# Recurrent stage of a decoder: the turned items regrouped into one row set and two channel groups

## The chip, the cores and the metric

The kernel runs on one core of a Trainium2 chip. The metric is the device time of one execution in microseconds. The five engines (TensorE or PE, VectorE or DVE, ScalarE or ACT, GpSimd or POOL, SyncE or SP) run their own instruction lists strictly in order and meet through semaphores; SyncE issues the transfers.

## The reference, cut to what matters

A two-layer decoder over 8 sequences of 256 tokens and 128 channels. Layer 0: linear attention, cross attention, a quantised feed-forward. Layer 1: four selective-scan (Mamba) blocks, cross attention with 16 heads of 64, a mixture of experts. Only the scan blocks matter here:

```python
dt = softplus(dbl[..., :64] @ dtw + dtb)
Bm, Cm = dbl[..., 64:80], dbl[..., 80:96]
A = -exp(A_log)
dA = exp(dt[..., None] * A)
dBu = (dt * u)[..., None] * Bm[:, :, None, :]
h = dA_t * h + dBu_t
y = einsum('ben,bn->be', h, C_t)
```

There are 256 inner channels and 16 states per channel, so each token has 4096 recurrences per block.

## The kernel before, in words

All of the change lies in `mamba_stage` (L1563 on). The work is cut into 16 **rounds** f (4 blocks times 4 quarters of 512 tokens, that is two sequences). While round f scans, the same engines prepare round F = f + 1 (projections, silu, softplus) and normalise the input of G = f + 2.

The 256 x 16 recurrences of a round are 16 **items** k, t = k % 16 being the place in the round. An item is a tile of 128 partitions x 1024: each partition holds one channel of a group of four (E32 = 32 channels by NI = 4 states), and the 1024 columns are two rows of 512 tokens. `place(k)` (L1604) says which: before, item t has channel half h = t // 8, row set pair np = (t // 4) % 2 and channel group q = t % 4; its two rows are two row sets of B and C (of NO = 4) for one channel group. Rows of dt and dt*u for the half are spread over the partitions by DMA (`dtR`, `dtuR`), rows of B and C likewise (`Bt`, `Ct`).

For an item the engines do: ScalarE `decay` (L2000), two exponentials of 512 columns with a scale per partition, into a PSUM pair that alternates by k % 2, so decay k waits for item k-2 to be done with its pair. GpSimd `times_b` (L1776), dt*u times B into one of eight slots of `hs`, three items ahead. VectorE `scan` (L2189), 1024 columns. Then the product with C, `times_c`, on VectorE for 9 items of a round (`NORM_D`, L1581) and on GpSimd (L1788) for the other 7: t = 0, 5, 9 to 13. TensorE `sum_y(f, j)` (L1861) folds the four items of batch j into a PSUM bank `Y[h]`, 8 matmuls, once all four products are there; VectorE `gate` multiplies the result of a half with silu(z).

Four items, t = 12 to 15, are **turned**: no GpSimd times_b. ScalarE makes scaled copies of the transposed dt*u (`scale_rows`, L2038, one per 128 tokens, state and row set: 32 a round, spread over the steps by `SCALED`), TensorE transposes them into the PSUM pair (`turn_rows`, L1914, 8 transposes an item), ScalarE writes their decays into `hs`, without a wait for the pair. `turn_b`/`copy_b` and `turn_dtu`/`copy_dtu` (L1900, L2025, L1906, L2032) make the transposed B and dt*u of the next round.

The order is written out by hand. ScalarE (L2124 on) does at step t: decay t+1, then what is due: `silus(F)` at 2 (two table loads, four silus), `x_rows` at 3, the softplus at 5, 6, 7, `copy_b` at 9, `square(G)` at 10, `residual(f-1)` at 11, `inv_std(G)` at 12, `affine(G)` at 14, `copy_dtu` at 15; then its scaled copies; then, at `KV_AT` = 4, 7, 12, 14 (L1654), one `kv_copy` (L2019): four times a round a tile of the next stage's keys or values, made by TensorE in a spare bank (`kv_job`, L1878), is brought to SBUF. VectorE (L2209) does scan, product, and `gate(f-1,1)` at 1, `step_size(F)` at 8, `gate(f,0)` at 9, `scaled_x(G)` at 13. GpSimd (L1805) does times_b t+3, times_c t, and `dt_times_u(F)` (L1794) at 8. TensorE's list (L1930 on) is, for a round: tap projection 0, sum_y(f-1,3), skip 0, tap projection 1, gate projection 0 (waits for `gate(f-1,1)`), gate projection 1 (waits for the first silu), x projection, kv_job, sum_y(f,0), dt projection, kv_job, sum_y(f,1), skip 1, turn_b (waits for `step_size`), centre(G), out_projection(f-1) (waits for `copy_b`), kv_job, turn_rows 12, average(G) (waits for `residual(f-1)`, since both use bank PA), turn_rows 13, sum_y(f,2), turn_rows 14, kv_job, turn_rows 15, turn_dtu.

## Time and profile before

| what | us |
|---|---|
| median of 3 runs | 1713.18 (1711.62 to 1714.34) |
| profiled execution, its own time | 1711.71 |
| its span, first to last instruction | 1710.0 |
| first scan starts, last product ends (in the span) | 501.86, 1318.14 |
| DVE busy over the span | 1387.7 |
| ACT busy over the span | 1312.0 |
| POOL busy over the span | 1074.3 |
| PE busy over the span | 1342.9 |

Busy times are sums of instruction durations on one engine; the clock of TensorE is given as a share of 2.4 GHz. In a timeline, "x2" merges instructions of one line and form that follow each other; the bracket is the engine's idle time before the row and what ended it. Round 8 (910.61 to 961.34) stands for the others: scan 0 of each round starts 50.7 us after the one before.

### The profile page before, as it was taken

The numbers are of one execution on the slowest core, as the hardware profiler recorded it, in microseconds if no ns is written. First come the engines' busy times: TensorE is split into PE (matmuls) and PEld (weight loads), VectorE is DVE, ScalarE is ACT, GpSimd is POOL, SyncE is SP. The second block draws the span as 40 slices with busy tenths as digits, with TensorE's granted clock in tenths as the row PEclk, the third lists the DMA queues.
The fourth block names the chain that finished last, engine by engine and source line by source line (L and its number), as shares of the span: only waits on it lengthen the run. The fifth ranks groups of instructions, "written<-read, shape, count | busy, mean of one in ns | idle before, by whom it ended". The sixth has DMA issues, their size and how long they took to land. (4 is left out here: it accounts for less than half of the span.)

```text
span 1710.0 us, 25211 instructions
## 1 busy us (share of the span) xinstructions
PE 1342.9 (79%) x7544; PEld 697.8 (41%) x7547; DVE 1387.7 (81%) x2394; ACT 1312.0 (77%) x2978; POOL 1074.3 (63%) x714
## 2 busy tenths in 40 slices
PE   6777898996677777877777777767766999899989
PEld 4554555653322222332222333222322466566543
DVE  3655788896529999999999999999997688778834
ACT  4444787884658999999999999999975787777730
POOL 2001566661048999999999999999995344444500
PEclk9999899998978889999988988999977999999979
DMA  3000000001045534455434545443530511121000
GB/s 105 2 1 2 1 2 2 1 2 26 7 174 203 179 124 173 167 205 199 168 136 162 203 157 199 177 160 129 192 142 25 185 50 50 62 87 50 2 0 25
DMA packets 70229, 168.19 MB, mean 98 GB/s; under 512 B 20420, under 2 KB 40152, under 8 KB 56664
## 3 DMA queue, kind: packets, MB, share of 16 engines
q1 hardware_dynamic: 68680, 166.17, 26.9%
q8 instruction: 55, 0.90, 0.2%
q10 hardware_dynamic: 1168, 0.53, 0.1%
q14 instruction: 70, 0.57, 0.1%
q0 software_dynamic: 256, 0.01, 0.0%
HBM read 131.04 MB, written 35.65 MB: 97 GB/s over the span
## 5 line engine op out<-in xcount | busy, mean ns | idle before, releaser
L1784 POOL TENSOR_TENSOR ma_hs<-ma_dtuR,ma_Bt 128x1024 f32<-128x1024 f32 x192 | 449.4, 2375 | 12.7 <-DMA ma_dtuR<-ma_dtu_d 6.7
L914 POOL TENSOR_TENSOR x_pr<-x_pr,x_rec 128x512 f32<-128x512 f32 x256 | 267.4, 1045 | 248.1 <-DVE x_rec L1202 248.1
L1161 ACT ACTIVATE x_pr<-x_sm,x_mx 128x256 f32<-128x256 f32 x512 | 255.3, 500 | 68.8 <-DVE x_mx L1193 65.7
L1867 PE MATMUL ps<-ma_hs,ma_fold 128*32 128x512 f32 x1024 | 157.7, 744 | 179.2 <-DVE ma_hs L2203 172.2
L2015 ACT ACTIVATE ps<-ma_dtR,ma_A 128x512 f32<-128x512 f32 x384 | 248.6, 680 | 48.6 <-DVE ma_hs L2203 41.6
L1792 POOL TENSOR_TENSOR ma_hs<-ma_hs,ma_Ct 128x1024 f32<-128x1024 f32 x112 | 264.3, 2371 | 22.2 <-DVE ma_hs L2197 22.2
L2197 DVE TENSOR_TENSOR_SCAN ps<-ps,ma_hs 128x1024 f32<-128x1024 f32 x112 | 255.9, 2285 | 7.9 <-ACT ps L2015 7.9
L2045 ACT ACTIVATE ma_rowB<-ma_dtuT,ma_BT 128x128 f32<-128x128 f32 x512 | 232.6, 524 | 1.3
L2197 DVE TENSOR_TENSOR_SCAN ma_hs<-ps,ma_hs 128x1024 f32<-128x1024 f32 x80 | 180.7, 2275 | 5.1 <-ACT ps L2015 5.1
L2203 DVE TENSOR_TENSOR ma_hs<-ps,ma_Ct 128x1024 f32<-128x1024 f32 x144 | 176.2, 1224 | 5.0
L990 PE MATMUL ps<-ident,x_pr 128*128 128x128 f32 x1024 | 161.6, 283 | 5.7 <-DVE x_pT L1073 4.3
L1867 PEld LDWEIGHTS ps<-ma_hs,ma_fold 128*32 128x32 f32 x1024 | 31.5, 125 | 274.3 <-DVE ma_hs L2203 210.5
L990 PEld LDWEIGHTS ps<-ident,x_pr 128*128 128x128 f32 x1024 | 113.2, 141 | 73.2 <-issue 52.9
L1193 DVE CUSTOM_DVE_ANT_0 x_sm<-x_sm,x_neg 128x256 f32<-128x256 f32 x256 | 111.6, 471 | 24.4 <-DVE x_sm L1189 24.4
L1834 PE MATMUL ps<-ma_hn,ma_w_tap 128*128 128x512 f32 (+3 forms) x256 | 118.6, 608 | 3.2 <-ACT ma_hn L2062 3.2
L1193 DVE CUSTOM_DVE_ANT_0 x_sm<-ps,x_mr 128x256 f32<-128x256 f32 x256 | 97.5, 418 | 22.4 <-PE ps L978 16.8
L1189 DVE TENSOR_TENSOR x_sm<-ps,x_m 128x512 f32<-128x512 f32 x128 | 86.6, 677 | 25.9 <-PE ps L978 25.5
L1161 ACT ACTIVATION_READ_ACCUMULATOR x_pr<-x_sm,x_mx 128x1 f32 x512 | 96.4, 188 | 0.0
L1073 DVE COPY x_pT<-ps 128x512 f32<-128x512 f32 x128 | 86.5, 676 | 5.0 <-PE ps L990 4.6
L1075 ACT ACTIVATE x_pT<-ps 128x512 f32<-128x512 f32 x128 | 74.7, 584 | 15.8 <-PE ps L990 14.3
L2015 ACT ACTIVATE ma_hs<-ma_dtR,ma_A 128x512 f32<-128x512 f32 x128 | 83.4, 716 | 0.0
L713 DVE TENSOR_TENSOR la_sc<-ps,la_tri 128x512 f32<-128x512 f32 x64 | 43.3, 680 | 48.2 <-PE ps L496 48.2
(325 smaller groups left out, 2598.8 us busy)
## 6 DMA issues: line engine op xcount, KB each, us to landing
ma_dtuR<-ma_dtu_d SPq DMA_DIRECT2D x32, 1024.0 KB, 6.7
ma_dtR<-ma_dt_d SPq DMA_DIRECT2D x32, 1024.0 KB, 6.6
ma_Bt<-ma_bc_d SPq DMA_DIRECT2D x16, 1024.0 KB, 4.9
ma_Ct<-ma_bc_d SPq DMA_DIRECT2D x16, 1024.0 KB, 7.4
ma_dtu_d<-ma_dtu SPq DMA_DIRECT2D x32, 256.0 KB, 2.0
ma_dt_d<-ma_dt SPq DMA_DIRECT2D x32, 256.0 KB, 2.3
keys_d<-ma_kv SPq DMA_DIRECT2D x32, 256.0 KB, 2.6
values_d<-ma_kv SPq DMA_DIRECT2D x32, 256.0 KB, 2.5
```

The costliest lines, as they stand in the source:

```text
L914: pool.tensor_tensor(pr[:, r, :, :], pr[:, r, :, :], rec[:, r, :].unsqueeze(2).broadcast_to([P, 2, L]), ALU.mult).then_inc(pr_done, 1)
L990: mm = pe.transpose(c.ps[:, 2 + n % 2, kt * L + t * P:kt * L + (t + 1) * P], pr[:, n % RP, t, kt * P:(kt + 1) * P], c.ident[:, :])
L1161: a = act.activation(pr[:, n % RP, t, :], sm[:, n % 2, t, :], ACT.Exp, bias=mx[:, n % 2, t:t + 1], scale=-1.0, accum_out=den[:, n % RP, t: ...
L1193: a = dve.tensor_tensor_reduce(sm[:, n % 2, t, :], bank[:, t, :] if small else sm[:, n % 2, t, :], mr[:, p, :] if small else neg[:, t, :], ...
L1784: pool.tensor_tensor(hs[:, k % SLOTS, :, :], dtuR[:, h, q, :].unsqueeze(1).broadcast_to([P, 2, CH]), rows(Bt, k), ALU.mult).then_inc(dbu_d ...
L1792: pool.tensor_tensor(hs[:, k % SLOTS, :, :], hs[:, k % SLOTS, :, :], rows(Ct, k), ALU.mult).then_inc(c_pool, 1)
L1834: mm = pe.matmul(out, w_tap[:, b, TAPS - 1 - e, h * P:(h + 1) * P], src, start=(e == 0), stop=(e == TAPS - 1), skip_group_check=True)
L1867: mm = pe.matmul(c.ps[q * E32:(q + 1) * E32, Y[h], :], fold[:, :], hs[:, (k0 + q) % SLOTS, a, :], start=False, stop=(j % 2 == 1 and a == 1 ...
L2015: e = act.activation(hs[:, k % SLOTS, a, :] if by_tensor(k) else c.ps[:, 2 * (k % 2) + a, :], dtR[:, h, q, :], ACT.Exp, scale=A[:, (f // Q ...
L2045: act.activation(rowB[:, t, a, :, :, ni], dtuT[:, t, :].rearrange("p (e q) -> p q e", q=GQ), ACT.Copy, scale=BT[:, f % 2, t, a, ni:ni + 1] ...
L2197: dve.tensor_tensor_scan(out, decays, inputs, 0.0, ALU.mult, ALU.add).then_inc(scan_done, 1)
L2203: dve.tensor_tensor(hs[:, k % SLOTS, :, :], c.ps[:, 2 * (k % 2):2 * (k % 2) + 2, :], rows(Ct, k), ALU.mult).then_inc(c_vector, 1)
```

## The change

- **Items.** An item is now one row set no and two channel groups (2qp, 2qp+1) of a half: `dtuR` gives two rows, B and C one row used twice. `ORDER` lists them: six items of half 0 (no 0 to 2), four of half 1 (no 0, 1), two of half 0 (no 3), four of half 1 (no 2, 3).
- **Turned items** are t = 10, 11 (half 0, no = 3) and 14, 15 (half 1, no = 3). All four use one row set, so 16 scaled copies of 256 columns (both halves) replace 32 of 128; `SCALED` spreads them over t = 0 to 8 and 15. `turn_dtu` transposes both halves into PA and PB (8 transposes), `copy_dtu` copies 1024 columns, at t = 14. `Bt` keeps three row sets.
- **Who makes the product with C**: GpSimd now for t = 0, 6, 8, 9, 12, 13, 14.
- **kv tiles**: copied at t = 0, 1, 4, 6; two jobs use Y[0] before skip 0, two Y[1] before skip 1. The two stores that stood behind Bt and Ct on SP's queue stand ahead of the wait for x_rows.
- **gate(f,0)** moves from t = 9 to t = 14, after sum_y(f,2), since half 0 now ends with item 11.
- TensorE's list follows; tap projection 0 now waits for `copy_dtu`.

```diff
@@ -1578,9 +1579,13 @@
     BIG = 1.0e24
-    NORM_D = set(range(16)) - {0, 5, 9, 10, 11, 12, 13}
-    TURNED = {12, 13, 14, 15}
-    SCALED = (3, 4, 0, 1, 2, 3, 3, 3, 3, 4, 3, 0, 0, 0, 0, 3)
+    NORM_D = set(range(16)) - {0, 6, 8, 9, 12, 13, 14}
+    TURNED = {10, 11, 14, 15}
+    SCALED = (2, 2, 0, 3, 2, 1, 0, 1, 2, 0, 0, 0, 0, 0, 0, 3)
+    FIRST, LAST_B, LAST = (0, 6), (5, 13), (11, 15)
+    ORDER = tuple((0, no, qp) for no in range(3) for qp in range(2)) + ((1, 0, 0), (1, 0, 1), (1, 1, 0), (1, 1, 1),
+                                                                        (0, 3, 0), (0, 3, 1), (1, 2, 0), (1, 2, 1),
+                                                                        (1, 3, 0), (1, 3, 1))
     xm = c.xn
@@ -1602,8 +1607,7 @@
-        s = k % ITEMS
-        return k // ITEMS, s // 8, (s // 4) % 2, s % 4
+        return (k // ITEMS,) + ORDER[k % ITEMS]
@@ -1620,10 +1624,10 @@
-        dtuT = s.sb("dtuT", [P, 4, P])
-        BT = s.sb("BT", [P, 2, 4, 2, NI])
+        dtuT = s.sb("dtuT", [P, 2, 4, P])
+        BT = s.sb("BT", [P, 2, 4, NI])
...
-        Bt = s.sb("Bt", [P, 2, NO, CH])
+        Bt = s.sb("Bt", [P, 2, NO - 1, CH])
@@ -1651,7 +1655,8 @@
         KV_K = 32
-        KV_AT = (4, 7, 12, 14)
+        KV_AT = (0, 1, 4, 6)
+        KV_BANK = (Y[0], Y[0], Y[1], Y[1])

@@ -1684,8 +1689,8 @@
-            f, _, np_, _ = place(k)
-            return tile[:, f % 2, 2 * np_:2 * np_ + 2, :]
+            f, _, no, _ = place(k)
+            return tile[:, f % 2, no, :].unsqueeze(1).broadcast_to([P, 2, CH])
@@ -1715,18 +1720,19 @@
+                    if f >= 0:
+                        kv_store(sp, 4 * f)
+                        kv_store(sp, 4 * f + 1)
...
+                        used = (NO - 1 + k) * CH
...
-                                     .broadcast_to([E32, NI, NO * CH])).then_inc(done, 16)
-                    if f >= 0:
-                        kv_store(sp, 4 * f)
-                        kv_store(sp, 4 * f + 1)
+                                     [:, :, 0:used].broadcast_to([E32, NI, used])).then_inc(done, 16)
@@ -1738,19 +1744,19 @@
-                        sp.wait_ge(dbu_done, n_times_b(f * ITEMS + 8))
+                        sp.wait_ge(dbu_done, n_times_b(f * ITEMS + LAST_B[0] + 1))
...
-                        sp.wait_ge(da_done, f * ITEMS + 8)
+                        sp.wait_ge(da_done, f * ITEMS + LAST[0] + 1)
...
-                        sp.wait_ge(dbu_done, n_times_b(f * ITEMS + 16))
+                        sp.wait_ge(dbu_done, n_times_b(f * ITEMS + LAST_B[1] + 1))
...
-                        sp.wait_ge(da_done, f * ITEMS + 16)
+                        sp.wait_ge(da_done, f * ITEMS + LAST[1] + 1)
@@ -1774,15 +1780,15 @@
-                    f, h, np_, q = place(k)
+                    f, h, _, qp = place(k)
...
-                    if k % 8 == 0:
+                    if k % ITEMS == FIRST[h]:
...
-                                       dtuR[:, h, q, :].unsqueeze(1).broadcast_to([P, 2, CH]),
+                                       dtuR[:, h, 2 * qp:2 * qp + 2, :],
@@ -1859,13 +1865,14 @@
-                    h = j // 2
...
-                    for a in range(2):
-                        for q in range(GQ):
-                            mm = pe.matmul(c.ps[q * E32:(q + 1) * E32, Y[h], :], fold[:, :], hs[:, (k0 + q) % SLOTS, a, :],
-                                           start=False, stop=(j % 2 == 1 and a == 1), skip_group_check=True)
+                    for k in range(k0, k0 + 4):
+                        _, h, _, qp = place(k)
+                        for a in range(2):
+                            q = 2 * qp + a
+                            mm = pe.matmul(c.ps[q * E32:(q + 1) * E32, Y[h], :], fold[:, :], hs[:, k % SLOTS, a, :],
+                                           start=False, stop=(k % ITEMS in (LAST[h] - 1, LAST[h])), skip_group_check=True)
@@ -1905,15 +1912,19 @@
                     if F + 1 < NF:
+                        pe.wait_ge(lnv_done, F + 2)
                         pe.wait_ge(scaled, F + 2)
+                    else:
+                        pe.wait_ge(resid, F - 1)
                     pe.wait_ge(dtu_done, 2 * F + 2)
-                    for a in range(4):
-                        mm = pe.transpose(c.ps[:, PB, a * P:(a + 1) * P], dtu[:, 1, a * P:(a + 1) * P], c.ident[:, :])
+                    for h, bank in ((0, PA), (1, PB)):
+                        for a in range(4):
+                            mm = pe.transpose(c.ps[:, bank, a * P:(a + 1) * P], dtu[:, h, a * P:(a + 1) * P], c.ident[:, :])
                     mm.then_inc(dtuT_ps, 1)
...
                 def turn_rows(k):
-                    f, h, np_, q = place(k)
-                    pe.wait_ge(rows_done, 32 * (f + 1))
+                    f, h, _, qp = place(k)
+                    pe.wait_ge(rows_done, 16 * (f + 1))
                     if on_vector(k - 2):
@@ -1921,7 +1932,7 @@
                             mm = pe.transpose(c.ps[:, 2 * (k % 2) + a, t * P:(t + 1) * P],
-                                              rowB[:, t, a, q, :, :].rearrange("p e n -> p (e n)"), c.ident[:, :])
+                                              rowB[:, t, h, 2 * qp + a, :, :].rearrange("p e n -> p (e n)"), c.ident[:, :])
                     mm.then_inc(turned, 1)
@@ -1930,40 +1941,45 @@
                 for f in range(-1, NF + 1):
                     F, G = f + 1, f + 2
                     if F < NF:
+                        if f >= 0:
+                            pe.wait_ge(dtuT_done, f + 1)
                         tap_projection(F, 0, PA)
                     if f >= 1:
                         sum_y(f - 1, 3)
                     if 0 <= f < NF:
-                        pe.wait_ge(dd_done, 2 * (f // QUARTERS) + 2)
                         if f >= 1:
                             pe.wait_ge(gated, 2 * f - 1)
-                            pe.wait_ge(kv_done, 4 * f)
-                        skip(f, 0)
+                        kv_job(4 * f, Y[0])
                     if F < NF:
-                        if f >= 0:
-                            pe.wait_ge(dtuT_done, f + 1)
                         tap_projection(F, 1, PB)
                         if f >= 1:
                             pe.wait_ge(gated, 2 * f)
                         gate_projection(F, 0, Y[1])
+                    if 0 <= f < NF:
+                        pe.wait_ge(kv_done, 4 * f + 1)
+                        kv_job(4 * f + 1, Y[0])
+                    if F < NF:
                         pe.wait_ge(u_done, 2 * F + 1)
                         gate_projection(F, 1, PA)
                         x_projection(F)
                     if 0 <= f < NF:
+                        pe.wait_ge(dd_done, 2 * (f // QUARTERS) + 2)
+                        pe.wait_ge(kv_done, 4 * f + 2)
+                        skip(f, 0)
                         if F < NF:
                             pe.wait_ge(z_done, 2 * F + 1)
                         else:
                             pe.wait_ge(gated, 2 * f)
-                        kv_job(4 * f, Y[1])
+                        kv_job(4 * f + 2, Y[1])
                         sum_y(f, 0)
                     if F < NF:
                         dt_projection(F)
                     if 0 <= f < NF:
-                        pe.wait_ge(kv_done, 4 * f + 1)
-                        kv_job(4 * f + 1, Y[1])
+                        pe.wait_ge(kv_done, 4 * f + 3)
+                        kv_job(4 * f + 3, Y[1])
+                        pe.wait_ge(kv_done, 4 * f + 4)
+                        skip(f, 1)
                         sum_y(f, 1)
-                        pe.wait_ge(kv_done, 4 * f + 2)
-                        skip(f, 1)
                     if F < NF:
                         pe.wait_ge(dt_done, 2 * F + 2)
                         turn_b(F)
@@ -1976,30 +1992,25 @@
                             pe.wait_ge(resid, f - 1)
                         out_projection(f - 1)
                     if 0 <= f < NF:
-                        pe.wait_ge(gated, 2 * f + 1)
-                        kv_job(4 * f + 2, Y[0])
-                    if 0 <= f < NF:
-                        turn_rows(f * ITEMS + 12)
+                        turn_rows(f * ITEMS + 10)
                     if G < NF:
                         if f >= 1:
                             pe.wait_ge(resid, f)
                         average(G)
                     if 0 <= f < NF:
-                        turn_rows(f * ITEMS + 13)
+                        turn_rows(f * ITEMS + 11)
                         sum_y(f, 2)
                         turn_rows(f * ITEMS + 14)
-                        pe.wait_ge(kv_done, 4 * f + 3)
-                        kv_job(4 * f + 3, Y[0])
+                    if F < NF:
+                        turn_dtu(F)
                     if 0 <= f < NF:
                         turn_rows(f * ITEMS + 15)
-                    if F < NF:
-                        turn_dtu(F)

             @block.scalar
             def _(act):
                 def decay(k):
-                    f, h, np_, q = place(k)
-                    if k % 8 == 0:
+                    f, h, no, qp = place(k)
+                    if k % ITEMS == FIRST[h]:
                         act.wait_ge(dt_in[h], 16 * (f + 1))
                     if k % (ITEMS * QUARTERS) == 0:
                         act.wait_ge(a_done, f // QUARTERS + 1)
@@ -2011,7 +2022,7 @@
-                        no = 2 * np_ + a
+                        q = 2 * qp + a
@@ -2025,15 +2036,16 @@
-                        act.wait_ge(rows_done, 32 * (F - 1))
-                    act.activation(BT[:, F % 2, :, :, :], c.ps[:, PA, 0:4 * 2 * NS].rearrange("p (t x n o) -> p t x o n", t=4, x=2, o=NO)
-                                   [:, :, 0, 2:4, :], ACT.Copy).then_inc(bT_done, 1)
+                        act.wait_ge(rows_done, 16 * (F - 1))
+                    act.activation(BT[:, F % 2, :, :], c.ps[:, PA, 0:4 * 2 * NS].rearrange("p (t x n o) -> p t x o n", t=4, x=2, o=NO)
+                                   [:, :, 0, NO - 1, :], ACT.Copy).then_inc(bT_done, 1)
...
-                        act.wait_ge(rows_done, 32 * F)
-                    act.activation(dtuT[:, :, :].rearrange("p t e -> p (t e)"), c.ps[:, PB, :], ACT.Copy).then_inc(dtuT_done, 1)
+                        act.wait_ge(rows_done, 16 * F)
+                    act.activation(dtuT[:, :, :, :].rearrange("p h t e -> p h (t e)"), c.ps[:, PA:PB + 1, :], ACT.Copy
+                                   ).then_inc(dtuT_done, 1)
@@ -2041,9 +2053,9 @@
-                    t, a, ni = i // 8, i // 4 % 2, i % 4
-                    act.activation(rowB[:, t, a, :, :, ni], dtuT[:, t, :].rearrange("p (e q) -> p q e", q=GQ), ACT.Copy,
-                                   scale=BT[:, f % 2, t, a, ni:ni + 1]).then_inc(rows_done, 1)
+                    t, ni = divmod(i, 4)
+                    act.activation(rowB[:, t, :, :, :, ni], dtuT[:, :, t, :].rearrange("p h (e q) -> p h q e", q=GQ), ACT.Copy,
+                                   scale=BT[:, f % 2, t, ni:ni + 1]).then_inc(rows_done, 1)
@@ -2150,7 +2162,7 @@
                             copy_b(F)
-                        if F < NF and t == 15:
+                        if F < NF and t == 14:
                             copy_dtu(F)
@@ -2161,7 +2173,7 @@
                         if t in KV_AT:
-                            kv_copy(4 * f + KV_AT.index(t), Y[1] if t < 9 else Y[0])
+                            kv_copy(4 * f + KV_AT.index(t), KV_BANK[KV_AT.index(t)])
                         if t == 14 and f % QUARTERS == 1 and f // QUARTERS + 1 < NBLK:
@@ -2182,7 +2194,7 @@
                 def gate(f, h):
-                    dve.wait_ge(y_done, 4 * f + 2 * h + 2)
+                    dve.wait_ge(y_done, 4 * f + h + 3)
                     zz = z[:, f % 3, h, :]
@@ -2220,10 +2232,10 @@
                             step_size(F)
-                        if t == 9:
-                            gate(f, 0)
                         if t == 13 and G < NF:
                             scaled_x(G)
+                        if t == 14:
+                            gate(f, 0)

```

## Rows read from the trace of the kernel before

**Rows 1.** The page, part 1: busy us of each engine, share of the span, instructions.

```profile
PE 1342.9 (79%) x7544; PEld 697.8 (41%) x7547; DVE 1387.7 (81%) x2394; ACT 1312.0 (77%) x2978; POOL 1074.3 (63%) x714
```

**Rows 2.** Windows: length, busy time and count by engine, clock, DMA share, GB/s.

```profile
911.80:962.50 50.70, 37.62 (x161) 14.98 (x154) 49.48 (x31) 47.57 (x87) 46.91 (x24) 0.90 0.49 180
```

**Rows 3.** Timeline of VectorE, round 8: start, duration, line, out<-in, [idle before <-releaser].

```profile
910.61 2.28 DVE L2197 TENSOR_TENSOR_SCAN ma_hs<-ps,ma_hs 128x1024 f32<-128x1024 f32 x1
912.81 2.27 DVE L2197 TENSOR_TENSOR_SCAN ps<-ps,ma_hs 128x1024 f32<-128x1024 f32 x1
...
916.26 0.68 DVE L2187 TENSOR_TENSOR ma_z<-ps,ma_z 128x512 f32<-128x512 f32 x1
...
924.20 2.30 DVE L2197 TENSOR_TENSOR_SCAN ps<-ps,ma_hs 128x1024 f32<-128x1024 f32 x1 [0.34 <-ACT ps L2015]
...
941.44 2.28 DVE L2197 TENSOR_TENSOR_SCAN ma_hs<-ps,ma_hs 128x1024 f32<-128x1024 f32 x1
...
954.40 2.29 DVE L2197 TENSOR_TENSOR_SCAN ps<-ma_hs,ps 128x1024 f32<-128x1024 f32 x1 [0.36 <-PE ps L1923]
...
957.87 2.29 DVE L2197 TENSOR_TENSOR_SCAN ps<-ma_hs,ps 128x1024 f32<-128x1024 f32 x1
...
961.34 2.28 DVE L2197 TENSOR_TENSOR_SCAN ma_hs<-ps,ma_hs 128x1024 f32<-128x1024 f32 x1
```

**Rows 4.** Timeline of ScalarE, round 8.

```profile
909.25 1.35 ACT L2045 ACTIVATE ma_rowB<-ma_dtuT,ma_BT 128x128 f32<-128x128 f32 x3
...
916.37 1.30 ACT L2015 ACTIVATE ps<-ma_dtR,ma_A 128x512 f32<-128x512 f32 x2
...
922.80 1.30 ACT L2015 ACTIVATE ps<-ma_dtR,ma_A 128x512 f32<-128x512 f32 x2
...
927.01 0.59 ACT L2023 ACTIVATE ma_kv<-ps 128x512 f32<-128x512 f32 x1
```

**Rows 5.** Timeline of TensorE, round 8; a product counts twice or more.

```profile
910.75 1.92 PE L1867 MATMUL ps<-ma_hs,ma_fold 128*32 128x512 f32 x16 [1.52 <-DVE ma_hs L2203]
...
913.57 3.58 PE L1834 MATMUL ps<-ma_hn,ma_w_tap 128*128 128x512 f32 x8
916.99 1.13 PE L1840 MATMUL ps<-ma_hn,ma_w_gate 128*128 128x512 f32 x2
...
936.92 3.64 PE L1867 MATMUL ps<-ma_hs,ma_fold 128*32 128x512 f32 x16 [8.14 <-DVE ma_hs L2203]
...
942.10 0.43 PE L1902 MATMUL ps<-ident,ma_xp 32*128 32x32 f32 x4
...
945.99 1.02 PE L1888 MATMUL ps<-ma_w_kv,cT 128*128 128x512 f32 x2
947.43 1.09 PE L1923 MATMUL ps<-ident,ma_rowB 128*128 128x128 f32 x8 [0.42 <-ACT ma_rowB L2045]
949.14 1.12 PE L1898 MATMUL ps<-ma_sq,average 128*128 128x512 f32 x2 [0.61 <-ACT xn L2083]
```

**Rows 6.** ScalarE by form: count, busy us, mean ns of one, idle before.

```profile
L2045 ACT ACTIVATE ma_rowB<-ma_dtuT,ma_BT 128x128 f32<-128x128 f32 x512 | 232.6, 524 | 1.3
...
L590 ACT ACTIVATE la_qm<-la_qk,la_member 128x256 f32<-128x256 f32 x64 | 28.4, 499 | 0.0
...
L1406 ACT ACTIVATE ffn_y<-ps,ffn_ht 128x128 f32<-128x128 f32 x16 | 5.1, 382 | 1.2 <-PE ps L1350 1.2
```

**Rows 7.** Timeline of GpSimd, round 8.

```profile
946.58 7.05 POOL L1792 TENSOR_TENSOR ma_hs<-ma_hs,ma_Ct 128x1024 f32<-128x1024 f32 x3 [0.41 <-DVE ma_hs L2197]
...
958.23 4.70 POOL L1784 TENSOR_TENSOR ma_hs<-ma_dtuR,ma_Bt 128x1024 f32<-128x1024 f32 x2
```

**Rows 8.** Timelines of TensorE (rounds 0 and 15) and VectorE (round 14).

```profile
512.36 2.08 PE L1840 MATMUL ps<-ma_hn,ma_w_gate 128*128 128x512 f32 x2 [4.02 <-ACT ma_u L2069]
...
1267.46 3.64 PE L1867 MATMUL ps<-ma_hs,ma_fold 128*32 128x512 f32 x16 [4.94 <-DVE ma_hs L2203]
...
1260.39 2.29 DVE L2197 TENSOR_TENSOR_SCAN ps<-ma_hs,ps 128x1024 f32<-128x1024 f32 x1 [2.94 <-PE ps L1923]
```

## The prediction

> **What bounds the kernel now.** I read the page first: VectorE is the busiest engine [rows 1]. Then the windows: in one round of the recurrent stage (0.8 ms of the span, sixteen rounds) VectorE is busy 49.48 of 50.70 us, ScalarE 47.57, GpSimd 46.91, TensorE 37.62 [rows 2]. So VectorE's list of sixteen scans sets the pace, and what can be won is its idle time alone, some 1.2 us a round. The timeline of VectorE shows where that sits [rows 3]: 0.34 us ahead of scan 4, released by ScalarE, and 0.55 us ahead of the turned scans, 0.36 of it ahead of scan 14, released by TensorE. An item whose product VectorE makes takes it 3.46 us (957.87 to 961.34), one whose product GpSimd makes 2.20 (910.61 to 912.81), a gate 0.6. Every microsecond by which another engine makes VectorE wait is lost for good. Round 8 is the pattern; T is the start of scan 0 (910.61), S the end of `step_size` (941.44, T + 30.8), X the start of scan 11.
>
> ScalarE's timeline says why scan 4 waits [rows 4]: decay 3 starts at T + 5.8, then come two table loads and four silus, decay 4 starts 6.43 us after decay 3 (922.80 - 916.37), and scan 4 follows its start by 1.40. TensorE takes its list strictly in order: it sits 8.14 us idle before `sum_y(1)`, whose first matmuls then last 3.64 us where 1.92 is usual [rows 5]. The granted clock averages 0.90 of 2.4 GHz over the round [rows 2]: a fifth of it ran at the lower level of 1.2 GHz, and that is where it lies.
>
> **Part 1: the scaled copies.** 32 copies of 128 columns a round become 16 of 256. One takes 524 ns, three take 1.35 us together [rows 4, 6]. A copy of 256 contiguous columns with a scale of the same kind takes 499 ns, one of 128 takes 382 [rows 6]; so the 256 strided ones lie between 0.45 us apiece and twice the old one, 0.9. I take 0.55, nearest to the old row plus the difference of the other two. ScalarE's busy time falls by 14.5 (232.6 / 16) - 8.8 = 5.7 us a round (bounds 0 and 7.3). ScalarE does not bound the round, so this is worth at most the 0.34 us ahead of scan 4, and only if nothing else makes decay 4 late. The Trainium skill (SBUF — State Buffer, section Door 1, the note on cachelines) says that consecutive accesses that each cross to a new 16-byte line pay a penalty. The copies step by 16 bytes on both sides; the excess of 524 over 382 ns agrees, and if that penalty is paid per element a copy would cost about 0.7 us by that rule, an estimate; only three copies lie on the path below, so the sum would move by under 0.5 us a round.
>
> **Part 2: kv copies at t = 0 and 1.** They were behind decays 5, 8, 13 and 15, where ScalarE had slack; now the first two stand before decay 2 and decay 3 in ScalarE's list.
> (a) kv_job 4f stands behind `sum_y(f-1,3)`, and that waits for item 14's product on GpSimd. Its list after scan 12 is now product 12, times_b 16, product 13, times_b 17, product 14: five instructions of 2.33 us [rows 7], 11.7 us from the end of scan 12 at X + 5.65, thus X + 17.3. Scan 0 of the next round would start at X + 14.7 (items 11 and 15 at 3.46, 12 to 14 at 2.20, a gate and a `scaled_x` at 0.6). So `sum_y` starts at T + 2.7 (before: T + 0.1), takes 1.9, the job 1.0, the copy 0.5 [rows 4, 5]: decay 2 starts at T + 6.2, scan 2 at T + 7.6 where it was 6.25.
> (b) kv_job 4f+1 stands behind the second tap projection (3.4) and behind a gate projection (1.0), which waits for `gate(f-1,1)` (done at T + 6.3). From T + 5.6: tap to 9.1, gate projection to 10.0, job to 11.1, copy to 11.6. Decay 3 starts there (before 5.8), scan 3 at T + 13.0, decay 4 at 11.6 + 6.43 = 18.0, scan 4 at T + 19.4 instead of 13.6.
> (c) TensorE is then idle from 11.1 until the first silu ends at 14.9, 3.8 us. In the first round it was idle 4.02 us there, and its gate projection took 2.08 instead of 1.13 us [rows 5, 8]. That adds 0.93: scan 4 at T + 20.35. Three copies and `x_rows` between decays 4 and 5 add 0.2. Together **7.0 us** later at S than now (5.8 with the clock at its upper level).
>
> **Part 3: the turned items are 10, 11, 14, 15 (were 12 to 15).** Their transposes stand where the old ones stood in TensorE's list.
> (a) `turn_rows(10)` is behind turn_b, centre and out_projection(f-1). turn_b waits for `step_size`, and with `sum_y(1)` at its 3.64 us it starts at S + 0.3. From turn_b to the end of out_projection is 945.99 - 942.10 = 3.9 us, the transposes 1.09 [rows 5]: scan 10 can start at S + 5.3. VectorE has only scan 9 to do after S and is free at S + 2.2. Before, four scans and a gate stood there. **3.1 us** lost.
> (b) `turn_rows(11)` is behind average(G), and that waits for residual(f-1) [rows 5], which on ScalarE stands behind decay 12. Decay 12 is now an ordinary one, so it waits for item 10's product: S + 5.3 + 3.46 = 8.8. Then decay 12 (1.2), residual (0.6, as the kv copy of rows 4), average (1.0) and transposes (1.0): scan 11 at S + 12.8, VectorE free at 8.8: 4.0 us. TensorE was idle 5.4 us before average; each idle of 4.9 us and more in this stage was followed by matmuls at the lower level [rows 5, 8]. With that, average and transposes take 2.0 us more: **5.9 us**.
> (c) After X, `turn_rows(14)` and `turn_rows(15)` are ready at X + 6.7 to 8.8 and X + 10.6 to 12 against VectorE's X + 8.45 and 11.25: 0.4 us. The 0.57 us that the turned scans waited before is gone.
>
> **Part 4: with one answer.** Scans (16), VectorE products (9), times_b (12) and GpSimd products (7) keep number and shape, the scan at 2.28, GpSimd's at 2.35 us [rows 3, 7]; a repeated row in place of two rows costs nothing, since times_b repeats one operand already and takes as long as the product that doesn't. `turn_dtu` has 8 transposes for 4 and `copy_dtu` 1024 columns for 512, each 0.5 us, before T and under scans 14 and 15. Bt's load is a quarter smaller; DMA engines are busy about half [rows 2]. On SP's queue dtR 0 now waits for decay 11, at S + 2.3, under the wait for dtu anyway; dtuR 1 waits for times_b 13 at S + 11, and is needed a round later; the kv stores that moved ahead of `xp_done` are done by then. If these were late, decay 16 or times_b 16 would wait; there are over 5 us of room.
>
> **Sum.** A full round (f = 1 to 13): 7.0 + 3.1 + 5.9 + 0.4 - 0.6 = 15.8, times 13 = 205. Round 0: 4.5 (no sum to wait for, but tap 0 now waits for copy_dtu). Round 14: 7.0 + 3.1 + 1.2 less the 2.94 us stall of before [rows 8] = 8.4. Round 15: 2.5 (no taps, no silus). Opening: 1. That is +221 us on the profiled execution's 1711.7: 1933. The median of the runs is 1.5 us above it, so 1934. About 0.2% (3 us) is what a measurement of this kernel tells from nothing.
>
> **Rivals.**
> - *The clock holds* at 2.4 GHz through the idle times of 3.8 and 5.4 us: 5.8 + 3.1 + 4.0 - 0.6 = 12.3 a round, 160 + 12: 1885. Against it: rows 8.
> - *The clock also falls in the 3.2 us before `sum_y(3)`*: sum and job 1.7 + 1.0 us longer, ahead of decay 3: 2.7 to 3.5 a round, 14 rounds: 1972 to 1982. For it: the shortest idle time followed by the lower level in this stage is 4.02, against it 1.5 us did no harm; nothing lies between.
> - *Only one of the two groups of waits holds* (part 2 hidden, or part 3): 13 x 8.8 + 5 gives 1833, 13 x 6.4 + 15 gives 1812. It needs an error of mine in one engine's order.
> - *Faster*: the halved copies take ScalarE out of the way, decay 4 comes early, and both stalls of rows 3 vanish: 16 x 1.0 + 2.9 + 1 = 20, 1694. This decides if the first two kv copies are ready when ScalarE comes to them, that is if kv_job 4f+1 ends by T + 5.2, one copy ahead of decay 3's start. Against it: it cannot start before the gate at T + 6.3. The Trainium skill (Perfetto Trace Analysis, Optimizing Scalar/DVE Operations) holds that fewer, larger operations raise throughput if the engine is saturated; at 47.57 of 50.70 us ScalarE is close to it, which is what speaks for this case.
> - *It changes nothing*: the copies gain what the waits cost: 1713.
>
> **How the numbers follow.** Forecast 0.50; clock holds 0.15; clock falls earlier too 0.22; one group only 0.07; faster 0.04; nothing 0.02. The forecast is the likeliest. Leaving out the last three (0.13) and little above 1985, the range is 1850 to 1985; its lower end lets 35 us of waits be smaller than in the clock-holds case. Faster 0.04, same 0.02, slower 0.94.
>
> **What would show it.** The page: VectorE busy time as before (1388 us), the span some 220 longer. VectorE's timeline in a middle round: period 66 us; idle ahead of scan 2 and 3 (1.4, 1.9), scan 4 (3 to 4) from ScalarE; ahead of scan 10 (3.1) and scan 11 (5.9) from TensorE's transposes. ScalarE: idle ahead of the kv copies, released by TensorE. The copies at L2045: 256 of them, near 0.6 us. TensorE's clock at 0.5 at average. Wrong if scan 11 follows scan 10's product at once, if the period is under 60 us, or if VectorE's own instructions got longer.

## The result, and the profile after

The changed kernel takes 1939.95 us (median of 4 runs, 1938.44 to 1940.37) against 1713.76 for the kernel before (4 runs): ratio 1.1321, 95% interval 1.1306 to 1.1336. The forecast was 1934, so the change is slower by what was said, within 6 us. The profiled execution took 1938.44, against 1711.71: +226.7 where the sum gave +221.

The page of the changed kernel, busy times (its row of [rows 1]):

```profile
PE 1446.3 (75%) x7608; PEld 743.0 (38%) x7611; DVE 1395.7 (72%) x2394; ACT 1274.3 (66%) x2722; POOL 1073.9 (55%) x714
```

ScalarE has 37.7 us less to do (1312.0 - 1274.3): 51.4 less in scaled copies, less what the doubled `copy_dtu` takes and what the records lose in overlap. GpSimd has the same. TensorE has 64 transposes more, four a round in `turn_dtu`, and is busy 103 us longer, most of it because more of its matmuls ran at the lower clock: the granted clock over the span is 0.871, against 0.922 before. VectorE's busy time is 8.0 us longer. 3.0 of that is in the durations of its instructions, which add up to 1532.6 us against 1529.6; the other 5 come from the records, in which an instruction that follows its predecessor at once overlaps it by some 0.08 us (in round 8 scan 1 starts at 1033.45, 0.09 us before scan 0 ends) and one that waited does not. Nearly all of the 227 us is idle time of VectorE.

The groups of VectorE by line, shapes apart, for the kernel before (count, busy us, mean ns, idle time just before them and what ended it):

```profile
L2197 DVE TENSOR_TENSOR_SCAN ps<-ps,ma_hs 128x1024 f32<-128x1024 f32 x112 | 255.9, 2285 | 7.9 <-ACT ps L2015 7.9
...
L2197 DVE TENSOR_TENSOR_SCAN ps<-ma_hs,ps 128x1024 f32<-128x1024 f32 x32 | 73.3, 2290 | 10.9 <-PE ps L1923 8.9 <-ACT ma_hs L2015 1.7
L2197 DVE TENSOR_TENSOR_SCAN ma_hs<-ma_hs,ps 128x1024 f32<-128x1024 f32 x32 | 72.7, 2277 | 4.5 <-PE ps L1923 1.9 <-ACT ma_hs L2015 1.7
```

The same groups of the changed kernel:

```profile
L2209 DVE TENSOR_TENSOR_SCAN ps<-ps,ma_hs 128x1024 f32<-128x1024 f32 x96 | 220.2, 2294 | 116.3 <-ACT ps L2026 110.7 <-POOL ma_hs L1790 3.8
...
L2209 DVE TENSOR_TENSOR_SCAN ps<-ma_hs,ps 128x1024 f32<-128x1024 f32 x48 | 110.0, 2291 | 118.2 <-PE ps L1934 118.2
...
L2209 DVE TENSOR_TENSOR_SCAN ma_hs<-ma_hs,ps 128x1024 f32<-128x1024 f32 x16 | 36.5, 2284 | 4.4 <-PE ps L1934 4.1
```

"ps<-ps,ma_hs" are ordinary items whose product VectorE makes: idle time ahead of them rises from 7.9 to 116.3 us, released by ScalarE's decays. "ps<-ma_hs,ps" and "ma_hs<-ma_hs,ps" are the turned items: from 15.4 to 122.6 us, released by TensorE's transposes. The gates add 4.8 (3.8 to 8.6). Together 220.4: the two places of the forecast, about half each.

Round 8 of the changed kernel (the same round as in [rows 3]), as a window (columns as in [rows 2]):

```profile
1031.26:1096.60 65.34, 43.13 (x158) 17.57 (x158) 49.88 (x32) 45.20 (x70) 46.39 (x23) 0.82 0.38 136
```

VectorE is busy 49.88 of 65.34 us. Its timeline in round 8, from scan 0 on, answers to [rows 3]:

```profile
1031.26 2.28 DVE L2209 TENSOR_TENSOR_SCAN ma_hs<-ps,ma_hs 128x1024 f32<-128x1024 f32 x1
...
1038.46 2.30 DVE L2209 TENSOR_TENSOR_SCAN ps<-ps,ma_hs 128x1024 f32<-128x1024 f32 x1 [0.88 <-ACT ps L2026]
...
1043.59 2.30 DVE L2209 TENSOR_TENSOR_SCAN ps<-ps,ma_hs 128x1024 f32<-128x1024 f32 x1 [1.57 <-ACT ps L2026]
...
1050.96 2.30 DVE L2209 TENSOR_TENSOR_SCAN ps<-ps,ma_hs 128x1024 f32<-128x1024 f32 x1 [3.82 <-ACT ps L2026]
...
1072.46 2.30 DVE L2209 TENSOR_TENSOR_SCAN ps<-ma_hs,ps 128x1024 f32<-128x1024 f32 x1 [2.83 <-PE ps L1934]
...
1081.73 2.30 DVE L2209 TENSOR_TENSOR_SCAN ps<-ma_hs,ps 128x1024 f32<-128x1024 f32 x1 [5.72 <-PE ps L1934]
...
1105.93 2.30 DVE L2209 TENSOR_TENSOR_SCAN ps<-ps,ma_hs 128x1024 f32<-128x1024 f32 x1 [2.57 <-ACT ps L2026]
```

These are scans 0, 2, 3, 4, 10 and 11, and scan 2 of the next round. Over the rounds 1 to 13, scan 3 waits 1.57 us in nearly every one, scan 10 2.83, scan 11 5.72; scan 2 changes between 0.8 and 3.2 from round to round. The means are 2.11, 1.58 and 3.47 (scans 2 to 4), 2.91 and 5.68 (scans 10, 11).

ScalarE's side of it (answers to [rows 4]):

```profile
1036.57 0.60 ACT L2034 ACTIVATE ma_kv<-ps 128x512 f32<-128x512 f32 x1 [2.54 <-PE ps L1895]
...
1041.70 0.60 ACT L2034 ACTIVATE ma_kv<-ps 128x512 f32<-128x512 f32 x1 [1.99 <-PE ps L1895]
1042.19 1.29 ACT L2026 ACTIVATE ps<-ma_dtR,ma_A 128x512 f32<-128x512 f32 x2
...
1049.56 1.30 ACT L2026 ACTIVATE ps<-ma_dtR,ma_A 128x512 f32<-128x512 f32 x2
...
1076.05 1.30 ACT L2026 ACTIVATE ps<-ma_dtR,ma_A 128x512 f32<-128x512 f32 x2 [5.74 <-DVE ma_hs L2215]
1077.29 0.57 ACT L2095 ACTIVATE xn<-ps 128x512 f32<-128x512 f32 x1
```

Both early kv copies (L2034) wait for TensorE, decay 3 (1042.19) stands behind the second, and decay 4 (1049.56) comes 7.37 us after decay 3. Further down decay 12 waits 5.74 us for item 10's product, and the residual (1077.29) behind it is what TensorE's average waits for:

```profile
1033.55 1.92 PE L1874 MATMUL ps<-ma_hs,ma_fold 128*32 128x512 f32 x16 [2.91 <-POOL ma_hs L1798]
1035.40 1.12 PE L1895 MATMUL ps<-ma_w_kv,cT 128*128 128x512 f32 x2
1036.37 3.58 PE L1840 MATMUL ps<-ma_hn,ma_w_tap 128*128 128x512 f32 x8
1039.78 1.02 PE L1846 MATMUL ps<-ma_hn,ma_w_gate 128*128 128x512 f32 x2
1040.64 1.02 PE L1895 MATMUL ps<-ma_w_kv,cT 128*128 128x512 f32 x2
1045.54 2.08 PE L1846 MATMUL ps<-ma_hn,ma_w_gate 128*128 128x512 f32 x2 [3.88 <-ACT ma_u L2081]
...
1071.38 1.04 PE L1934 MATMUL ps<-ident,ma_rowB 128*128 128x128 f32 x8
1077.91 2.07 PE L1905 MATMUL ps<-ma_sq,average 128*128 128x512 f32 x2 [5.49 <-ACT xn L2095]
1079.78 1.91 PE L1934 MATMUL ps<-ident,ma_rowB 128*128 128x128 f32 x8
...
1099.37 3.25 PE L1874 MATMUL ps<-ma_hs,ma_fold 128*32 128x512 f32 x16 [3.17 <-POOL ma_hs L1798]
```

Here is the list that the prediction wrote down: sum (L1874), kv job (L1895), tap (L1840), gate projection (L1846), kv job, then 3.88 us idle and a gate projection of 2.08 us where one takes 1.02 to 1.13. The transposes of item 10 (1071.38) stand behind `out_projection`, average (1077.91) waits 5.49 us, and it and item 11's transposes run at double length.

### The profile page after: what moved, and what is told of

Its sections match the earlier page's. It is cut to its first block and busy times, and to the rows that moved or that the text cites. A ratio compares the mean times of both kernels' runs of the same rounds, so it can differ in the third digit from the quotient of the medians.

```text
span 1936.7 us, 25067 instructions
## 1 busy us (share of the span) xinstructions
PE 1446.3 (75%) x7608; PEld 743.0 (38%) x7611; DVE 1395.7 (72%) x2394; ACT 1274.3 (66%) x2722; POOL 1073.9 (55%) x714
## 5 line engine op out<-in xcount | busy, mean ns | idle before, releaser
L2209 DVE TENSOR_TENSOR_SCAN ps<-ps,ma_hs 128x1024 f32<-128x1024 f32 x96 | 220.2, 2294 | 116.3 <-ACT ps L2026 110.7
L1874 PE MATMUL ps<-ma_hs,ma_fold 128*32 128x512 f32 x1024 | 186.3, 865 | 127.2 <-DVE ma_hs L2215 75.0
L2209 DVE TENSOR_TENSOR_SCAN ma_hs<-ps,ma_hs 128x1024 f32<-128x1024 f32 x96 | 217.1, 2276 | 5.1 <-ACT ps L2026 5.1
L2209 DVE TENSOR_TENSOR_SCAN ps<-ma_hs,ps 128x1024 f32<-128x1024 f32 x48 | 110.0, 2291 | 118.2 <-PE ps L1934 118.2
L2057 ACT ACTIVATE ma_rowB<-ma_dtuT,ma_BT 128x256 f32<-128x256 f32 x256 | 181.2, 762 | 0.1
L1874 PEld LDWEIGHTS ps<-ma_hs,ma_fold 128*32 128x32 f32 x1024 | 35.5, 140 | 247.6 <-issue 139.0
L1840 PE MATMUL ps<-ma_hn,ma_w_tap 128*128 128x512 f32 (+3 forms) x256 | 121.2, 618 | 10.5 <-ACT ma_dtuT L2047 7.3
L1865 PE MATMUL ps<-ma_u,ma_dD 128*128 128x512 f32 x64 | 50.6, 884 | 71.3 <-ACT ma_kv L2034 71.3
L2034 ACT ACTIVATE ma_kv<-ps 128x512 f32<-128x512 f32 x64 | 37.9, 592 | 96.6 <-PE ps L1895 48.4
L1934 PEld LDWEIGHTS ps<-ident,ma_rowB 128*128 128x128 f32 x512 | 73.4, 168 | 49.1 <-issue 48.6
```

Source lines behind the costliest of these rows:

```text
L1840: mm = pe.matmul(out, w_tap[:, b, TAPS - 1 - e, h * P:(h + 1) * P], src, start=(e == 0), stop=(e == TAPS - 1), skip_group_check=True)
L1874: mm = pe.matmul(c.ps[q * E32:(q + 1) * E32, Y[h], :], fold[:, :], hs[:, k % SLOTS, a, :], start=False, stop=(k % ITEMS in (LAST[h] - 1, L ...
L2057: act.activation(rowB[:, t, :, :, :, ni], dtuT[:, :, t, :].rearrange("p h (e q) -> p h q e", q=GQ), ACT.Copy, scale=BT[:, f % 2, t, ni:ni ...
L2209: dve.tensor_tensor_scan(out, decays, inputs, 0.0, ALU.mult, ALU.add).then_inc(scan_done, 1)
```

## The experiments

Twelve kernels ran. The kernel before ran beside each set, at 1712.6, 1713.6 and 1712.0 us.

**The kv copies moved back (e1_kv).** In the changed kernel:

```diff
-        KV_AT = (0, 1, 4, 6)
-        KV_BANK = (Y[0], Y[0], Y[1], Y[1])
+        KV_AT = (3, 4, 5, 6)
+        KV_BANK = (Y[0], Y[1], Y[1], Y[1])
```

with the jobs of the first two behind `x_projection` in TensorE's list. The copies then stand ahead of decays 5 to 8.

> The changed kernel with its four kv copies moved from t = 0, 1, 4, 6 to t = 3, 4, 5, 6, and the first two jobs behind x_projection in TensorE's list. My theory (part 2 of the prediction): the idle ahead of scans 2, 3 and 4, about 7.6 us a round, comes from ScalarE standing at the first two copies; some 1 us of it stays, since sum_y(f-1,3) is still late. 14 rounds by 6.5 us: 1850 us (1840 to 1862), idle ahead of scan 10 and 11 as in the changed kernel (2.8 and 5.7). Rival: ScalarE is late for another reason (the dearer scaled copies of 762 ns, five of which stand before decay 3), and the idle ahead of scan 4 stays: 1900 or more.

Measured: 1893.24 (ratio 1.1055, 1.1036 to 1.1073), 47 us less than the change where 90 were expected. The waits ahead of scans 2 and 3 are nearly gone; in most rounds scan 4 keeps 2.18 us and scan 5 has 0.55, scan 7 has 2.54 where it had under 0.1, and the gates wait 6.9 us more over the span. Why scan 4 does, TensorE and ScalarE show (timelines of this kernel):

```profile
1009.57 3.64 PE L1874 MATMUL ps<-ma_hs,ma_fold 128*32 128x512 f32 x16 [3.18 <-POOL ma_hs L1798]
1013.14 4.86 PE L1840 MATMUL ps<-ma_hn,ma_w_tap 128*128 128x512 f32 x8
```

```profile
1018.04 0.69 ACT L2078 ACTIVATE ma_u<-ps,ma_vec 128x512 f32<-128x512 f32 x1 [2.40 <-PE ps L1840]
...
1031.67 0.60 ACT L2100 ACTIVATE ma_dtu<-ps 128x512 f32<-128x512 f32 x1 [1.61 <-PE ps L1860]
```

The sum that waits for GpSimd's product of item 14 comes after 3.18 us of idle time and takes 3.64, the tap behind it 4.86 where 3.58 is usual, and so the second silu waits 2.40. At 1031.67 the softplus waits 1.61 for `dt_projection`, which stood behind a skip that waited for a kv copy. So my repair left one cause in (the late sum) and brought one of its own: the waits ahead of scan 7 add up to 35.3 us where they were 1.2. The 47 us are therefore what the repair won less what it cost, and no measure of the early copies; the next run is that. What this run does show is that the late sum, at the lower clock, is enough to hold up scan 4 without them.

**The same copies put into the kernel before (b1_kv01).** `KV_AT = (0, 1, 12, 14)` the first two jobs at the changed kernel's places, and skip 0, which shares their bank, behind `x_projection` as there; nothing else of the change.

> The kernel before, with one thing taken over from the change: the first two kv copies of a round stand ahead of decays 2 and 3 instead of behind decays 5 and 8, their TensorE jobs stand where the changed kernel has them, and skip 0 behind x_projection. Item order, turned items, scaled copies and products stay as before. Theory of the early copies: job 4f now stands behind sum_y(f-1,3), ready near T+3.1, job 4f+1 behind the gate projection, ready near T+8.4; decay 3 starts 2.6 us later, scan 4 between 3 and 4 us later than its 13.6, in 14 rounds: 50 us slower, 1765 (1750 to 1780). Rival, the scaled copies' gain was what the changed kernel needed the order for, and ScalarE's own list is the limit: with the heavier list of before the copies hide nothing, and it costs over 80 us, above 1795. Rival, the early copies matter only together with the new item order: 1713 to 1720.

Measured: 1764.31 (1.0295, 1.0278 to 1.0312), 51 us over the kernel before. Scans 3 and 4 in its VectorE timeline, and the matmul behind the idle time:

```profile
1003.86 2.30 DVE L2200 TENSOR_TENSOR_SCAN ps<-ps,ma_hs 128x1024 f32<-128x1024 f32 x1 [0.50 <-ACT ps L2018]
...
1011.23 2.30 DVE L2200 TENSOR_TENSOR_SCAN ps<-ps,ma_hs 128x1024 f32<-128x1024 f32 x1 [3.82 <-ACT ps L2018]
```

```profile
1005.81 2.08 PE L1840 MATMUL ps<-ma_hn,ma_w_gate 128*128 128x512 f32 x2 [3.88 <-ACT ma_u L2072]
```

In this kernel `sum_y(f-1,3)` is on time (T + 0.14), the items are in the old order and the copies are 32, and yet scan 4 waits 3.82 us, as in the changed kernel, behind the same 3.88 us of TensorE idle and a gate projection at 2.08. The early copies and their jobs cost this by themselves; neither the new order of the items nor the new scaled copies are needed for it. In four of the rounds 1 to 14 the gate projection after the same 3.88 us took 1.12 to 1.16 us, and there scan 4 waited 2.87 to 2.90: 0.9 of its wait is the clock.

**The transposes moved ahead (e2a_turn10, e2b_turn11, e2_rows).** Item 10's ahead of `turn_b`, item 11's ahead of `average`, each alone and both:

```diff
+                    if 0 <= f < NF:
+                        turn_rows(f * ITEMS + 10)
                     if F < NF:
                         pe.wait_ge(dt_done, 2 * F + 2)
                         turn_b(F)
...
                         out_projection(f - 1)
-                    if 0 <= f < NF:
-                        turn_rows(f * ITEMS + 10)
+                    if 0 <= f < NF:
+                        turn_rows(f * ITEMS + 11)
                     if G < NF:
                         if f >= 1:
                             pe.wait_ge(resid, f)
                         average(G)
                     if 0 <= f < NF:
-                        turn_rows(f * ITEMS + 11)
```

> The changed kernel with turn_rows 10 ahead of turn_b and turn_rows 11 ahead of average in TensorE's list, nothing else. My theory (part 3): the idle of 2.8 us ahead of scan 10 and of 5.7 us ahead of scan 11 is the order of that list. Both go: 13 rounds by 8.5 us and 5 us in rounds 14 and 15: 1825 us (1815 to 1840). Rival: the turned items wait for the scaled copies or for decays, so that the idle stays in another place: 1900 or more.

> The changed kernel with only the transposes of item 10 moved, ahead of turn_b. Theory: part 3a by itself, 2.8 to 3.8 us of idle ahead of scan 10 gone; item 10's product, decay 12, residual and average come earlier by as much, and the wait ahead of scan 11 stays at 5.7: 13 rounds of 3 to 4.8: 1877 to 1900. Rival, VectorE's earlier item 10 only lengthens the wait ahead of scan 11 (TensorE bound by out_projection): above 1920.

> The changed kernel with only the transposes of item 11 moved, ahead of average. Theory: part 3b by itself, the wait ahead of scan 11 falls from 5.7 us to under 0.5, average and with it scaled_x and the next taps move later but stay covered by the items after it: 13 rounds of 5.3: 1866 to 1872. Rival, average, squares and the next round's taps come later, and 2 us of it shows at the next scans 2 to 4: near 1895.

Measured: both 1825.15 (1.0648, 1.0624 to 1.0672), item 10 alone 1878.59 (1.0981, 1.0957 to 1.1005), item 11 alone 1870.10 (1.0915, 1.0897 to 1.0933). Part 3 is thus 115 us of the 226: 61 and 70 by themselves. With both moved, the group of ordinary scans and that of the turned scans:

```profile
L2210 DVE TENSOR_TENSOR_SCAN ps<-ps,ma_hs 128x1024 f32<-128x1024 f32 x96 | 220.2, 2294 | 118.7 <-ACT ps L2027 109.6 <-POOL ma_hs L1790 6.8
...
L2210 DVE TENSOR_TENSOR_SCAN ps<-ma_hs,ps 128x1024 f32<-128x1024 f32 x48 | 109.6, 2283 | 6.3 <-PE ps L1934 6.3
```

The turned scans' idle time falls from 118.2 to 6.3 us. Little of it comes back: the other group has 118.7 for 116.3, the gates 13.5 for 8.6. With item 10 alone, scan 10's wait goes, and scan 11's falls to 3.94 in seven of the 13 rounds and to 4.40 in the mean (5.67 before), since TensorE now waits 1.9 to 2.5 us ahead of average in place of 5.49 and in 11 of them average takes 1.12 to 1.25 us. So the expectation that scan 11 would keep its 5.7 was wrong, though the time lay in its range. The 1.3 us a round at scan 11, 17 in 13 rounds, is also in e2b's gain, which is why the two alone add up to 131 and not to 115.

**TensorE kept busy ahead of average (e3_fill).** Item 11's transposes run five extra times, their results overwritten by the counted ones, between item 10's transposes and the wait for the residual; the order of everything else stays. It measures part 3's clock term alone.

> The changed kernel with five extra runs of the eight transposes of item 11, into the PSUM pair that turn_rows 11 overwrites later, between turn_rows 10 and the wait of average: TensorE works 4.4 of the 5.5 us in which it sat idle. No wait is taken away. My theory: the clock stays at 2.4 GHz, average and turn_rows 11 take 2.0 instead of 4.0 us, the idle ahead of scan 11 falls from 5.7 to 3.8 us in 13 rounds: 1915 us (1905 to 1925). Rival: the slower matmuls there have nothing to do with the idle time before them: 1940, or above it where the extra work delays average.

Measured: 1923.56 (1.1238, 1.1216 to 1.1260), 16 us less. The row of average in TensorE's timeline, with the fill ahead and item 11's transposes behind, and scan 11:

```profile
1061.84 5.18 PE L1934 MATMUL ps<-ident,ma_rowB 128*128 128x128 f32 x46
1068.15 1.13 PE L1905 MATMUL ps<-ma_sq,average 128*128 128x512 f32 x2 [1.12 <-ACT xn L2099]
1069.11 1.04 PE L1934 MATMUL ps<-ident,ma_rowB 128*128 128x128 f32 x8
```

```profile
1070.18 2.29 DVE L2213 TENSOR_TENSOR_SCAN ps<-ma_hs,ps 128x1024 f32<-128x1024 f32 x1 [3.94 <-PE ps L1934]
```

Average takes 1.13 us and the transposes 1.04 (2.07 and 1.91 without the fill), and scan 11 waits 3.94 us in place of 5.72. The clock term is 1.7 to 1.8 us a round, 23 in 13 rounds. Over the whole span the turned scans wait 21.2 us less (101.4 against 122.6), the ordinary ones 2.1 and the gates 2.3 more; that leaves the 16.

**Item 14's product on VectorE, item 4's on GpSimd (e4_prod).** One number of the set in `NORM_D`, 14 for 4.

> The changed kernel with the product with C of item 14 on VectorE and that of item 4 on GpSimd: each engine makes as many as before. My theory (part 2a): sum_y(f-1,3) starts at T + 0.1 instead of T + 2.9, the idle ahead of scan 2 (0.9 to 2.8 us) and of the gate (0.3 to 0.9) goes, that ahead of scan 3 falls from 1.6 to 0.6, that ahead of scan 4 stays above 2.9: 14 rounds by 3.6 us: 1890 us (1880 to 1905). Rival: ScalarE's wait for the second kv copy hides it all, since that waits for the gate anyway: 1930 or more.

Measured: 1910.28 (1.1157, 1.1139 to 1.1176), 30 us less where 50 were expected. Three scans of one round:

```profile
1026.89 2.30 DVE L2209 TENSOR_TENSOR_SCAN ps<-ps,ma_hs 128x1024 f32<-128x1024 f32 x1 [0.50 <-ACT ps L2026]
...
1034.26 2.29 DVE L2209 TENSOR_TENSOR_SCAN ma_hs<-ps,ma_hs 128x1024 f32<-128x1024 f32 x1 [3.81 <-ACT ps L2026]
1038.22 2.30 DVE L2209 TENSOR_TENSOR_SCAN ps<-ps,ma_hs 128x1024 f32<-128x1024 f32 x1 [1.67 <-ACT ps L2026]
```

These are scans 3, 4 and 5: the wait ahead of scan 2 is gone and scan 3's is 0.50, but scan 4 keeps its 3.8, and 1.67 us appear ahead of scan 5, which item 4's product on VectorE (1.23 us) had covered. So (a) of part 2 is shown: the late sum is the late product. Moving the product takes away some cover elsewhere: scan 5 waits 23.2 us over the span, and 2.6 in the changed kernel.

**Relief for ScalarE alone (b2_half).** The kernel before, 16 of its 32 scaled copies a round cut to four columns from round 1 on; the rows of the second row set then keep round 0's values.

> The kernel before, in its own order, with 16 of the 32 scaled copies of a round cut down to four columns from round 1 on (those of the second row of each pair; the rows they would write keep the values of round 0, so that part of the products of the turned items is left out). It measures what relief of ScalarE is worth by itself: 16 copies of 0.45 to 0.52 us become 16 of about 0.2, some 4 to 5 us a round. Theory: ScalarE does not bound the round, only the wait ahead of scan 4 (0.34 us) and part of the wait for the turned transposes can go: 4 to 10 us in all, 1704 to 1710. Rival, ScalarE is so close to the bound that relief is worth more, all 1.2 us of idle time a round: 1694. Rival, nothing: 1713.

Measured: 1706.58 (0.9958, 0.9942 to 0.9975). The page, and the scans of ordinary items:

```profile
PE 1334.3 (78%) x7544; PEld 698.7 (41%) x7547; DVE 1386.4 (81%) x2394; ACT 1263.1 (74%) x2978; POOL 1074.1 (63%) x714
```

```profile
L2201 DVE TENSOR_TENSOR_SCAN ps<-ps,ma_hs 128x1024 f32<-128x1024 f32 x112 | 255.9, 2285 | 7.9 <-ACT ps L2015 7.9
```

ScalarE has 48.9 us less to do, about what the change spares it in copies (51.4, below), and the wait of 0.34 us ahead of scan 4 has not moved: the group keeps its 7.9 us. The rounds keep their length, 50.73 us (1027.83 to 1078.56, scan 4 to scan 4). The whole stage is 2.4 us shorter, from the first scan at 504.76 to the last product's end at 1318.62; the waits of its scans and gates add up to 32.0 us against 32.2. The rest of the 5 to 7 us lies outside the stage and isn't explained, and of the 2.4 us 1.6 are in round 15, which is not a full one. So the expectation, that the wait ahead of scan 4 could go, was wrong, though the time lay in its range; and what the change was to gain was 2 to 7 us at most.

**Both repairs, and three more (e5c_kv_rows, e6c_all, e7c_all_s, e8_scaled).** e5c has e1's and e2's edits and `dt_projection` ahead of skip 0; e6c adds e4's; e7c spreads the copies of e6c anew; e8 is e5c with

```diff
-    SCALED = (2, 2, 0, 3, 2, 1, 0, 1, 2, 0, 0, 0, 0, 0, 0, 3)
+    SCALED = (3, 2, 0, 0, 2, 1, 0, 1, 2, 0, 0, 0, 0, 0, 0, 5)
```

> The changed kernel with both repairs: kv copies ahead of decays 4 to 7 (jobs behind x_projection, dt_projection ahead of skip 0), and the transposes of items 10 and 11 ahead of turn_b and of average. If the gains of the two repairs add (47 and 115 us were measured singly, and the order of dt_projection should give about 5 us more): 1940 - 167 = 1773. If the two also free each other (no idle time over 3 us on TensorE ahead of a released instruction, so the clock holds more often): 1735 to 1750. Rival, what one repair wins the other loses, as the filling transposes did: above 1800.

> As the run with both repairs, and item 14's product on VectorE, item 4's on GpSimd. Theory: the product of item 14 at the end of GpSimd's five instructions holds up sum_y(f-1,3), the second tap projection and the silus; without it 25 us less than the run with both repairs (singly it brought 30). Rival, GpSimd's product of item 4 then comes late for decay or sum of the first batch and the gain is under 10 us.

> As the run before this one, with the scaled copies spread otherwise over the round: two fewer ahead of decays 1 and 3, none moved to the turned items, more behind items 0, 6 and 7. Theory: ScalarE's list between decay 3 and decay 4 is now what holds scan 4, two copies less there are 1.5 us: 10 to 20 us less than the run before, under 1713 if that one is under 1728. Rival, TensorE's taps hold it: the same time within 4 us.

> As the run with both repairs (1748), with the scaled copies of the round spread (3, 2, 0, 0, 2, 1, 0, 1, 2, ..., 5): the three between decay 4 and decay 5 done earlier, while ScalarE still waits for VectorE. Theory: what holds scans 3, 4 and 6 (33 us of idle time) is ScalarE's own list behind the silus; three copies less there are 2.2 us a round, of which the waits ahead of scans 5 and 6 gain 0.6: 10 us less, 1738. Rival, the copies moved forward delay decay 3 as much: 1748 or up to 10 more.

Measured: 1747.96 (1.0200, 1.0183 to 1.0217), 1753.79 (1.0235), 1747.83 (1.0194) and 1736.32 (1.0138, 1.0113 to 1.0162).

e5c: both repairs take 192 of the 226 us back, 30 more than the two apart (47 and 115). Scan by scan, e1's 2.54 us ahead of scan 7 are 0.6 (`dt_projection` no longer stands behind the skip), and its 2.2 ahead of scan 4 are 0.2 to 1.6. Over the span scan 7's waits are 7.4 us where e1 had 35.3. These 28 us are the cost that e1 had brought with it, and the expectation had 5 for it; so the time fell into the range of 1735 to 1750 for another reason than the one given there, that the repairs free each other.

e6c was a miss, 6 us more where 25 less were expected: the waits for GpSimd's `times_b`, 7.0 us in e5c, are gone, but what ScalarE releases late, over all ordinary scans, rises from 32.4 to 57.0, 20.7 of it ahead of scan 5, which item 4's product had covered.

e7c is 6 us below e6c where 10 to 20 were expected. It brought ScalarE's part to 34.7, and lost part of it ahead of the turned scans (11.1 to 26.4). Its theory had misread `SCALED`: no copy stood between decays 3 and 4. Two of those that it moved stood between decays 4 and 5, and it was scan 5 that gained (1.85 to 0.54 us a round).

e8 came within 2 us of its number. Scans 5 and 7 gained 14.4 us together; scan 4, one of those said to be held by ScalarE's list, gained none (14.2 and 15.1 us). The groups of e5c and of e8,

```profile
L2207 DVE TENSOR_TENSOR_SCAN ps<-ps,ma_hs 128x1024 f32<-128x1024 f32 x96 | 219.8, 2290 | 33.8 <-ACT ps L2024 26.7 <-POOL ma_hs L1790 7.0
...
L2207 DVE TENSOR_TENSOR_SCAN ps<-ma_hs,ps 128x1024 f32<-128x1024 f32 x48 | 109.7, 2286 | 18.1 <-PE ps L1934 16.7 <-ACT ps L2024 1.3
```

```profile
L2207 DVE TENSOR_TENSOR_SCAN ps<-ps,ma_hs 128x1024 f32<-128x1024 f32 x96 | 219.4, 2285 | 21.4 <-ACT ps L2024 15.2 <-POOL ma_hs L1790 6.3
...
L2207 DVE TENSOR_TENSOR_SCAN ps<-ma_hs,ps 128x1024 f32<-128x1024 f32 x48 | 109.9, 2289 | 22.1 <-PE ps L1934 21.8
```

ScalarE's part falls from 26.7 to 15.2 us, the turned scans' rises by 4.0. No version of the changed kernel beat the kernel before; e8, the best, is 1.4% slower. In e8 the scans and gates wait 60.6 us in all, in the kernel before 32.2; whether a further order of TensorE's list removes the rest wasn't tried.

## Why the prediction was right

Its terms for a full round beside the measured ones (means over rounds 1 to 13, from VectorE's idle time ahead of each scan; part 2 less the 0.34 us of before). Two errors in part 2 cancel, as said below; that its 7.0 came so close is luck in part:

| step | predicted | measured |
|---|---|---|
| part 2: scans 2 to 7 and the gates | 7.0 | 7.4 |
| part 3a: scan 10 | 3.1 | 2.9 |
| part 3b: scan 11 | 5.9 | 5.7 |
| part 3c and what was there before | -0.2 | -0.4 |
| sum | 15.8 | 15.5 |

- **Part 1, the copies.** Mis-sized. By form, the changed kernel's row of [rows 6]:

```profile
L2057 ACT ACTIVATE ma_rowB<-ma_dtuT,ma_BT 128x256 f32<-128x256 f32 x256 | 181.2, 762 | 0.1
```

One record lasts 762 ns in the mean, and three that follow each other take 2.06 to 2.12 us together, 0.69 apiece where I took 0.55; I had leaned on the difference of two contiguous forms (499 - 382). The kernel's copies went from 232.6 to 181.2 us, a gain of 51.4 or 3.2 us a round, and not 5.7. The Trainium skill (SBUF — State Buffer, section Door 1, on cachelines) says that accesses that each cross to a new 16-byte line pay a penalty; the estimate drawn from it, 0.7, was the better value, and the trace agrees with it. The relief was worth next to nothing either way, as b2_half shows.
- **Part 2a.** Sum at T + 2.3 (2.7 predicted), first kv copy at T + 5.3, scan 2 at T + 7.2 (7.6), in round 8 with T = 1031.26: right.
- **Part 2b and c.** Decay 3 at T + 10.9 (11.6), decay 4 at 18.3 (18.95 with the clock term), scan 4 at 19.7 (20.35). TensorE idle 3.88 us (3.8) in every round: right, and b1_kv01 shows the part of the early copies by itself. The clock term of (c), 0.93 us, was right in six of the rounds 1 to 13 alone, where the gate projection took 2.07 or 2.08 as in this one. In five it took 1.32 to 1.77, and in two, rounds 5 and 12, 1.12 at the full clock after the same 3.88 us (the row of round 5 is shown in the last section). In the mean it cost 0.6.
- **The rival of the early clock** was true in some rounds. After 2.91 us of idle time `sum_y(3)` took 1.92 us (1033.55), after 3.17 one round on it took 3.25 (1099.37), and scan 2 then waited 2.57 us and not 0.88. I gave it 0.22, as all or nothing; it came in 9 of 13 rounds (the sum takes 2.92 to 3.64 us, and scan 2 waits over 2), and cost less than priced: in those rounds the gate projection after the 3.88 us mostly ran faster, and scan 4 waits less (2.87 to 3.52 in most, and not 3.82). So the mean of scan 2 is 2.11 where the sum had 1.35, and that made up for a clock term of (c) that was too large in the mean and for a scan 4 that came 0.65 us sooner, in round 8, than in it. The forecast had the clock fall at one place in every round; it fell at either of two. The order of the list, not this, was what it had right. Nor was it so that nothing lay between 1.5 and 4.02 us of idle time in the trace of before: at 541.12 transposes took 1.10 us after 1.99, and at 496.83, ahead of the first scan, four ran at 0.50 after 2.17.
- **Part 3.** Both terms as predicted and shown by e2a, e2b and e2_rows; the clock's share of 3b by e3_fill, 1.7 to 1.8 us where the sum had 1.9.
- **The whole, by length.** The first scan starts 1.3 us later (1 predicted). Round 0 is 6.9 us longer (4.5), rounds 1 to 13 207.9 (205), round 14 9.1 (8.4), round 15 up to the last product 4.4 (2.5). What follows the last product is 2.8 us shorter, which the sum did not have and no run explains. Together that is 226.7. In rounds 1 to 13 a round is 16.0 us longer (66.7 and 50.7), and the waits of the table are 15.5 of them; the other 0.5 us is in no term: it is what VectorE loses in overlap and in slightly longer instructions at its new waits.
- **Faster**, the rival: it needed the first two kv copies ready by T + 5.2. They came at T + 5.3 and T + 10.4. The Trainium skill (Perfetto Trace Analysis, Optimizing Scalar/DVE Operations) has it that fewer, larger operations can raise throughput if the engine is saturated. ScalarE, at 94% of a round, was not the one that bound it: 48.9 us of relief gave 2.4 us in the stage.

## What to carry to other kernels

Where one engine's list is nearly full, cost an edit by what each instruction will stand behind in the other engines' lists, one by one; that gave the mean waits here within 0.8 us. Work taken off an engine that only looked full was worth next to nothing (49 us of ScalarE gave 2 to 7), while a move of two 0.6 us copies and their jobs a few places ahead cost 51. Where an item's input comes from TensorE, look at which waits stand ahead of it in TensorE's list that have nothing to do with it: two sets of transposes put ahead of such a wait, and not behind it, were worth 115 us. And a repair can bring a wait of its own, as e1, e4 and e6c did; read the scans one by one before taking its gain for the size of a cause.

## What the runs showed of the hardware

- **TensorE's clock after 3 to 4 us of idle time.** The same product after the same wait ran at either level. In the changed kernel, the gate projection of round 5, whose row in round 8 is shown above (1045.54, 2.08 us, granted clock 0.50):

```profile
845.99 1.12 PE L1846 MATMUL ps<-ma_hn,ma_w_gate 128*128 128x512 f32 x2 [3.88 <-ACT ma_u L2081]
```

After 3.88 us idle it took 1.12 us at a granted clock of 1.00 of 2.4 GHz, in round 8 it took 2.08 at 0.50, that is 1.2 GHz. In the run with both repairs, `sum_y(f-1,3)` of round 10, and a skip and a later sum of the same round (TensorE, and the windows of the two sums, with the clock behind the busy times):

```profile
1042.40 1.92 PE L1874 MATMUL ps<-ma_hs,ma_fold 128*32 128x512 f32 x16 [3.18 <-POOL ma_hs L1798]
...
1065.05 2.08 PE L1865 MATMUL ps<-ma_u,ma_dD 128*128 128x512 f32 x2 [1.61 <-ACT ma_kv L2032]
1069.21 3.64 PE L1874 MATMUL ps<-ma_hs,ma_fold 128*32 128x512 f32 x16 [2.09 <-POOL ma_hs L1798]
```

```profile
1042.40:1044.30 1.90, 1.90 (x17) 0.52 (x17) 1.87 (x2) 1.90 (x4) 1.90 (x3) 1.00 0.04 9
1069.20:1072.80 3.60, 3.58 (x17) 0.69 (x17) 3.60 (x4) 2.54 (x4) 2.68 (x2) 0.50 0.00 0
```

After 3.18 us idle the sum of round 10 took 1.92 us at 1.00; that of round 8 took 3.59 after 3.17 us (935.08), and in e1_kv it took 3.64 after 3.18. The later sum took 3.64 at 0.50 after only 2.09 us idle. There the clock had fallen before that wait: the skip at 1065.05, after waits of 2.22 and 1.61 us, already took 2.08 where the one at 1055.99 took 1.10. So the length of the last idle stretch alone doesn't say which level follows. What decides it, these runs do not show.
- **A ScalarE copy in steps of 16 bytes** takes 762 ns for 256 columns, 524 for 128 and 290 for four (the cut ones of b2_half), so 1.86 ns a column between 128 and 256 and 1.89 between four and 128, against 0.91 for contiguous copies ((499 - 382) / 128), of which the shorter one reads PSUM and not SBUF.
